# LayerNorm of the tokens along partitions, on a host-transposed copy, in place of TensorE's token transpositions

## What is computed

```python
def _layernorm(x, axis=-1, eps=1e-05):
    m = jnp.mean(x, axis=axis, keepdims=True)
    v = jnp.var(x, axis=axis, keepdims=True)
    return (x - m) / jnp.sqrt(v + eps)
...
q = (x @ w_q)   # of _layernorm(x)
k = (context @ w_k)
v = (context @ w_v)
sim = jnp.einsum('bhid,bhjd->bhij', q, k) * SCALE
out = einsum('bhij,bhjd->bhid', softmax(sim), v)
...
x = x + _L0_xattn_ref(_layernorm(x, axis=-1), ctx_768, L0_xattn_w_q, L0_xattn_w_k, L0_xattn_w_v, L0_xattn_w_o, L0_xattn_b_o)
x = x + _L0_ffn_ref(_layernorm(x, axis=-1), L0_ffn_gate, L0_ffn_W1, L0_ffn_b1, L0_ffn_W2, L0_ffn_b2)
```

## Time and profile before

| | |
|---|---|
| median of 3 runs | 1581.21 us (1580.75 to 1581.81) |
| the profiled execution | 1580.22 us, its span 1578.5 us |
| PE busy | 1553.8 us, 98% |
| PE weight load | 1454.0 us, 92% |
| DVE busy | 1176.1 us, 75% |
| ACT busy | 1108.0 us, 70% |
| POOL busy | 818.1 us, 52% |
| mean TensorE clock granted | 0.994 |
| moved by DMA | 145.05 MB, 92 GB/s |

### The profile page before, as it was taken

The page is one execution under the profiler, slowest core; times in us unless marked ns, Lnnn a source line. Parts: engine busy times, 40 slices in busy tenths (PEclk is TensorE's granted clock), DMA queues, the critical chain, the costliest instruction groups (busy, mean ns, idle before and its releaser), DMA issues.

```text
span 1578.5 us, 45424 instructions
## 1 busy us (share of the span) xinstructions
PE 1553.8 (98%) x14150; PEld 1454.0 (92%) x14151; DVE 1176.1 (75%) x3796; ACT 1108.0 (70%) x3357; POOL 818.1 (52%) x946
## 2 busy tenths in 40 slices
PE   8999999999999999999999999999999999999997
PEld 7899999999899999999999989998899999999997
DVE  4777777777777777777777777777788777777775
ACT  5677677677776777767767777676666676777774
POOL 2344545545554554554555455455456555555556
PEclk9999999999999999999999999999999999999999
DMA  6522111222111221211122211122799755555554
GB/s 201 145 72 74 60 60 60 77 90 72 62 60 60 67 94 66 74 60 60 63 75 89 74 60 60 60 67 81 241 231 249 144 86 85 89 86 90 84 84 61
DMA packets 105643, 145.05 MB, mean 92 GB/s; under 512 B 12736, under 2 KB 87616, under 8 KB 105344
## 3 DMA queue, kind: packets, MB, share of 16 engines
q1 hardware_dynamic: 60144, 89.00, 17.8%
q0 software_dynamic: 26816, 37.32, 13.7%
q10 hardware_dynamic: 18640, 18.19, 4.4%
HBM read 77.09 MB, written 67.38 MB: 92 GB/s over the span
## 4 chain that ended last, share of the span: by engine, by line
issue 47%; POOL 22%; PE 9%; DVE 7%; DMA 6%; DVEq 3%; ACT 2%; POOLq 2%; ACTq 1%; SPq 0%
POOL lists L662 7%; DMA out<-stage_room,number 6%; PE bank_a L1404 4%; POOL prob L669 3%; DVE hid L1332 3%; POOL rstd L648 2%; DVE stage_room L1349 2%; POOL stage_room L711 2%; POOL stage_room L707 2%; POOL out L735 2%; DVEq L1344 1%; PE bank_v L1437 1%; POOLq L729 1%; PE bank_s L1422 1%; DVEq L1323 1%
## 5 line engine op out<-in xcount | busy, mean ns | idle before, releaser
L669 POOL TENSOR_TENSOR prob<-prob,inv 128x512 f32<-128x512 f32 x256 | 271.4, 1060 | 520.3 <-DVE inv L956 519.6
L777 ACT ACTIVATE prob<-bank_s,low 128x128 f32<-128x128 f32 x1024 | 363.3, 376 | 40.9 <-DVE low L951 40.9
L735 POOL DMA_INDIRECT out<-stage_room,number x142 | 231.8, 1632 | 53.9 <-issue 53.1
L951 DVE TENSOR_REDUCE low<-bank_s 128x4 f32<-128x512 f32 x256 | 175.4, 685 | 98.0 <-PE bank_s L1422 97.9
L777 ACT ACTIVATION_READ_ACCUMULATOR prob<-bank_s,low 128x1 f32 x1024 | 221.1, 216 | 0.0
L770 ACT ACTIVATE probt<-bank_t 128x512 f32<-128x512 f32 x256 | 153.4, 599 | 89.6 <-PE bank_t L1411 89.6
L1050 DVE SCALAR_TENSOR_TENSOR stage_room<-xin,wo_t 128x256 f32<-128x256 f32 x480 | 178.8, 426 | 0.0
L807 ACT ACTIVATE ot_h<-bank_v 128x512 fp32r<-128x512 f32 x128 | 77.4, 604 | 138.4 <-PE bank_v L1437 138.4
L885 ACT ACTIVATE hidt_h<-hid 128x512 fp32r<-128x512 f32 x142 | 89.7, 632 | 117.4 <-DVE hid L1332 112.2
L1411 PE MATMUL bank_t<-ident,prob 128*128 128x128 f32 x1024 | 161.9, 281 | 4.0 <-POOL prob L669 4.0
L1404 PE MATMUL bank_a<-xt_l,wq_h 128*128 128x256 f32 x512 | 152.4, 298 | 0.3 <-DVE xt_l L966 0.3
(11 more groups left out here) (231 smaller groups left out, 4728.9 us busy)
## 6 DMA issues: line engine op xcount, KB each, us to landing
stage_room<-lists ACTq DMA_DIRECT2D x67, 265.0 KB
halves<-stage_room SPq DMA_DIRECT2D x32, 512.0 KB
homes<-halves SPq DMA_DIRECT2D x16, 1024.0 KB, 6.4
xin<-in_x SPq DMA_DIRECT2D x32, 256.0 KB, 2.8
stage_room<-in_x SPq DMA_DIRECT2D x32, 256.0 KB
stage_room<-in_w SPq DMA_DIRECT2D x32, 256.0 KB, 4.3
out<-stage_room SPq DMA_DIRECT2D x32, 256.0 KB, 2.2
cin<-in_ctx SPq DMA_DIRECT2D x32, 128.0 KB, 2.6
```

Source lines behind the costliest of these rows:

```text
L669: pool.tensor_tensor(prob[:, n % 4, :, :], prob[:, n % 4, :, :], wide(inv[:, n % 4, :], P), ALU.mult).then_inc(s_norm.sem, 1)
L735: pool.indirect_dma_start(out, bass.IndirectOffsetOnAxis(ap=number[:, u, b:b + 1], axis=0), ysum[:, u, b, :], None, compute_op=ALU.add).th ...
L777: e = act.activation(prob[:, n % 4, h, :], bank_s[n % 2][:, h * P:(h + 1) * P], ACT.Exp, bias=low[:, n % 4, h:h + 1], scale=-1.0, accum_ou ...
L951: dve.tensor_reduce(low[:, n % 4, :], bank_s[n % 2][:, :].rearrange("p (h k) -> p h k", h=4), AX.X, ALU.min).then_inc(s_low.sem, 1)
```

## The change

The host hands over a second, transposed copy of the tokens, `x_t`. SP loads it for each pair into `xraw` (features on partitions). Statistics and `rstd` are made as before, from `xin`, with `rstd` written into `mean_var` beside the mean. As mean and `rstd` are now wanted along the free axis on all partitions, SP writes the 2 x 2 numbers of each partition to DRAM (`ln_rows`) and reads them back broadcast to all partitions as `ln_all` (128x512: per token block and token the mean and `rstd`, so that the mean of one token lies four elements from that of the next). DVE then subtracts and multiplies over `xraw`, two instructions of 128x512, in slot 3, ahead of emptying o1; ACT copies `xraw` to `xt_h` in slot 4, behind `copy_t` and ahead of `exps`; DVE takes the low part from `xraw` in slot 4 where it took it from the bank. t0 is gone, and with it one of 16 users of `bank_a`; the banks now stand in a table. In the first iteration PE spreads the statistics by four products with `ident` instead.

```diff
     A_SLOTS = [
...
-        [("o1", FROM0), ("t0", NEXT)],
+        [("o1", FROM0)],
...
+    BANK_OF = {"q10": 0, "k10": 1, "o0": 2, "k11": 3, "q11": 0, "o1": 1, "v10": 2, "v11": 3,
+               "q00": 0, "k00": 1, "q01": 2, "k01": 3, "v00": 1, "f0": 0, "v01": 2}
...
+            def ln_through(sp, it):
+
+                if not isinstance(it, int) or it > 0:
+                    sp.wait_ge(ln_in, it * 16)
+                wait(sp, pool_step, it, "rstd1")
+                sp.dma_start(ln_rows, mean_var[:, 0, :, :]).then_inc(ln_out, 16)
+                sp.wait_ge(ln_out, it * 16 + 16)
+                wait(sp, xn_step, it - 1, "xn")
+                sp.dma_start(ln_all.rearrange("p t b k -> p (t b k)"), ln_rows.rearrange("t b k -> (t b k)").rearrange(
+                    "(o n) -> o n", o=1).to_broadcast([P, 4 * P])).then_inc(ln_in, 16)
...
+                    sp.dma_start(xraw.rearrange("p c b t -> p c (b t)"),
+                                 x_t[:, cols].rearrange("(c p) t -> p c t", p=P)).then_inc(xt_in, 16)
...
                         wait(sp, c_lo, it - 1, "c")
-                        wait(sp, ln1_step, it - 1, "ln1")
+                        wait(sp, xa_lo, it - 1, "x")
+                        wait(sp, ln1_step, it - 1, "bn1_1")
...
                         load_x(it)
+                        ln_through(sp, it)
...
+                        if n == 4 and has(it, NEXT):
+
+                            wait(act, a_full, it, "q11")
+                            wait(act, xn_step, it, "xn")
+                            act.activation(xt[0][:, 0:DC, :], xraw.rearrange("p c b t -> p c (b t)"),
+                                           ACT.Copy).then_inc(xa_hi.sem, 1)
...
+                def of_tokens(it, k):
+
+                    if isinstance(it, int) and it == -1:
+                        rows_wide = bank_s[1][:, 2 * k * P:(2 * k + 2) * P].rearrange("p (b t) -> p b t", b=2)
+                    else:
+                        rows_wide = ln_all[:, :, :, k].rearrange("p t b -> p b t")
+                    return rows_wide.rearrange("p (o b) t -> p o b t", o=1).to_broadcast([P, DC, 2, P])
+
+                def normalise_turned(it):
+                    dve.wait_ge(xt_in, (it + 2) * 16)
+                    if isinstance(it, int) and it == -1:
+                        dve.wait_ge(ln_first, 1)
+                    else:
+                        dve.wait_ge(ln_in, it * 16 + 16)
+                    dve.tensor_tensor(xraw[:, :, :, :], xraw[:, :, :, :], of_tokens(it, 0), ALU.subtract).then_inc(xn_step.sem, 1)
+                    wait(dve, xn_step, it, "centred")
+                    dve.tensor_tensor(xraw[:, :, :, :], xraw[:, :, :, :], of_tokens(it, 1), ALU.mult).then_inc(xn_step.sem, 1)
+
+                def low_of_tokens(it):
+                    wait(dve, xa_hi, it, "x")
+                    dve.tensor_tensor(xt[1][:, 0:DC, :], xraw.rearrange("p c b t -> p c (b t)"),
+                                      xt[0][:, 0:DC, :].bitcast(F32), ALU.subtract).then_inc(xa_lo.sem, 1)
...
+                        if n == 3 and has(it, NEXT) and not (isinstance(it, int) and it < 0):
+                            normalise_turned(it)
...
+                        if n == 4 and has(it, NEXT):
+                            low_of_tokens(it)
                         made_in = it - 1 if n == 0 else it
...
-                        if n == 1 and has(it, NEXT):
-                            normalise(it, 0, xin, [xn[:, 0, :], xn[:, 1, :]])
...
-                        if k == 0:
-                            wait(pe, a_done, it if g == 0 else it - 1, "t0")
+                        if name == "q00":
+                            wait(pe, xa_lo, it, "x")
```

More of the change, by code:

```diff
@@ L130, in program @@
         [("o1", FROM0)],
[L131 removed]
+        [("v10", CUR), ("v11", CUR)],
         [],
@@ L225, in program @@
             cin = place("cin", 2, 2 * P)
-            xn = place("xn", 2, D)
-            place("not_used", WORK + HOME - taken_to[0])
+            xraw = place("xraw", DC, 2, P)
+            ln_all = place("ln_all", P, 2, 2)
+            assert taken_to[0] == WORK + HOME
             qt = place("qt", 2, CHUNKS // 2, 2 * P)
@@ L359, in by_products, with a_bank @@
                 return isinstance(it, int) and it < 1
[L361 to L367, removed]
+            def a_bank(name):
+                return bank_a[BANK_OF[name]]
             def bank_before(it, name):
+                same = [n for n, _ in A_EVENTS if BANK_OF[n] == BANK_OF[name]]
                 if not isinstance(it, int):
[L372 to L376, removed]
+                    k = same.index(name) - 1
+                    return (it if k >= 0 else it - 1), same[k]
+                order = [(j, n) for j in range(-1, PAIRS + 1) for n in a_full.present(j) if n in same]
+                k = order.index((it, name)) - 1
                 return order[k] if k >= 0 else (it, None)
@@ L647, in rstd_of @@
                     wait(pool, pool_step, it, f"shift{k + 1}")
-                    pool.tensor_tensor(rstd[:, k, :], shifted[:, k, :], mhalf[:, :],
+                    pool.tensor_tensor(mean_var[:, 0, :, 1] if k == 0 else rstd[:, k, :], shifted[:, k, :], mhalf[:, :],
                                        ALU.pow).then_inc(pool_step.sem, 1)
@@ L958, in second_part @@
                 def second_part(it, name):
-                    src = a_bank(it, name)
+                    src = a_bank(name)
                     kind, k = name[0], int(name[-1])
[L961 to L968, removed]
+                    wait(dve, a_full, it, name)
+                    if kind == "v":
                         last = dve.tensor_copy(vv[:, int(name[1]), k, :], src[:, :])
@@ L1035, in rows_of @@
                     dve.wait_ge(sent, (it - 1) * 64 + 16)
-                    normalise(it, 1, x1, [rows[:, b, 0:D] for b in range(2)])
+                    normalise(it, x1, [rows[:, b, 0:D] for b in range(2)])
                 def x_scores(it, first, many):
@@ L1128, in body @@
                             wait(dve, ln1_step, it, "bn1_1")
+                            if not isinstance(it, int) or it > 0:
+                                dve.wait_ge(ln_out, it * 16)
+                            elif it == 0:
+                                dve.wait_ge(ln_first, 1)
                         if n == 4 and has(it, PREV):
@@ L1448, in product @@
                         wait(pe, a_hi if of[0] in "qk" else a_done, earlier, of)
[L1449 to L1455 removed]
+                    if kind == "q":
                         g = int(name[1])
[L1457 to L1458 removed]
+                        if name == "q00":
+                            wait(pe, xa_lo, it, "x")
                         for j in range(2):
@@ L1567, in keep_busy, with first_statistics @@
                                   skip_group_check=True)
+                def first_statistics():
+                    wait(pe, pool_step, -1, "rstd1")
+                    pe.wait_ge(made, 20)
+                    for k in range(2):
+                        for b in range(2):
+                            last = pe.matmul(bank_s[1][:, (2 * k + b) * P:(2 * k + b + 1) * P],
+                                             mean_var[:, 0, b, k:k + 1].to_broadcast([P, P]), ident[:, :],
+                                             start=True, stop=True, skip_group_check=True)
+                    last.then_inc(ln_first, 1)
                 def gate_means():
@@ L1587, in _ @@
                 keep_busy(3)
-                pe.wait_ge(made, 20)
+                first_statistics()
                 iterations(pe, body)
```

56 lines of the change are left out of this document (26 added, 30 removed).

## The result

The changed kernel takes 1593.28 us at the median of 6 runs (1589.35 to 1595.74), the kernel before 1581.71 us beside it (1580.75 to 1582.68): a ratio of 1.0072, 95% interval 1.0058 to 1.0085. It is slower. The profiled execution took 1589.35 us, its span 1587.6 us against 1578.5 us. It is the fastest of the six runs, so of the 11.6 us between the medians its trace can account for some 9.

The account below looks back on a forecast made before the run. PE was taken to bound the loop: 0.86 us stall minus 0.44 us gained gives +0.42 us, 12.6 us over 30 iterations; with 0.6 us at the start 1593.4 us profiled, 1594.4 us median; range 1576 to 1613 us.

Parts of the forecast that it names:

- its own sign: Prediction counts as wrong if ACT gets to the tokens' high part before 2.28 us after u4's scores, or idle time stands elsewhere.
- the stall: PE before k00, waiting for the context's low part from DVE: 0.86 us an iteration, bounds 0.6 and 1.0 us.
- Bottleneck: Attention loop: PE is busy throughout, so work leaving its stream saves time and any wait of PE adds time.
- t0's worth: PE between an output sum's last product and `values`: 0.44 us an iteration gained, 31 x 0.44 = 13.6 us.
- The transfers: Statistics' DRAM round trip in the loop: 2.8 us each way, 2.3 us room, costed at nothing; `xraw` load at start, 0.6 us.
- Slot 3: DVE's subtraction and multiplication before o1: 0.60 us each from start to start, plus waiting with POOL; o1 0.15 to 0.2 us late.
- S: Zero point of the times within an iteration: the start on PE of the scores for u4 and u5.
- Exclusion with POOL: DVE with two SBUF operands and POOL reading SBUF exclude each other; the later waits, as with a `norm` of 1.04 us.
- The late high part: ACT, slot 4: tokens' high part starts behind `copy_t` 2.28 us after u4's scores, ends at 2.91, delaying DVE's low part and k00.
- S's: Wait before u3's transposes, by the experiments' theory that DVE's slot 3 is too long through 16-byte step and exclusion with POOL.
- the restart: PE at k00: the first product behind a wait takes 0.11 us more, 0.39 against the usual 0.28 us.
- rival A: Slot 3: four-element stride makes both DVE instructions 1.22 us, transposes 1.2 us late; 1606 us, or 1624; chance 0.20.

Follow-up runs that it names:

- the best version: Changed kernel with statistics 8 bytes apart, slot 3 of DVE free of gate products (X_SCORES 1: (0, 11), 2: (11, 3), 5: (14, 2)), high part early: 1571.15 us, ratio 0.9938.

## Why the prediction came out as it did

The time was right, 1594.4 against 1593.28 us (for the profiled execution 1593.4 against 1589.35 us); by what it was made of, half of it was not. By its own sign, idle time that stands elsewhere than before k00, its account of the stall is wrong.

- **Bottleneck, and t0's worth: right.** PE had no slack, `values` moved up by 0.44 us an iteration, an iteration in which nothing waits takes 33.73 us instead of 34.16, and the best version gets 9.9 of the 13.6 us.
- **The transfers: right.** Costed at nothing in the loop, and nothing waits for them: the write and its wait took 1.5 us at the median where 2.8 was put. At the start the first minimum came 0.30 us later (23.60 to 23.90), where 0.6 was put.
- **Slot 3: the step that failed.** "A `tensor_tensor` of this size takes DVE 0.60 us from start to start": taken from rows whose operands lie side by side. With one operand read 16 bytes apart it takes 1.07 us, and 1.10 us from start to start (0.70 and 0.69 us at 8 bytes apart). The forecast had o1 0.15 to 0.2 us late; it was 0.83 us late (660.82 against some 659.99, 0.32 behind its last product as in the kernel before). The minimum came at S + 2.14 instead of the forecast's S + 1.56. The exclusion was in the sum and the step was not; with the step taken away, or the exclusion, the wait before the transposes is gone.
- **Exclusion with POOL: right.** The multiplication of 1.85 us that is 1.08 us without `norm` shows it, as does `norm` itself: 1.53 us beside the low part.
- **The late high part: right and hidden.** It came at S + 2.28 as forecast (663.19). Its wait before k00 appears wherever S's is taken away, with 0.38 to 0.54 us of idle time. It is smaller than forecast because the minimum of u4 is earlier there, at S + 1.3 to S + 1.5 and not at S + 1.56: in the kernels with 8 bytes, with the products moved, with the short `norm` and with slot 3 free and the high part late, k00 starts 4.98 or 4.99 us behind that minimum (S + 6.30 behind S + 1.32 up to S + 6.49 behind S + 1.50). Behind S + 1.56 this gives S + 6.54, where the forecast had it before the restart (6.49 and 0.05). The term was sized right, but for a slip of 0.03 us: 6.49, 0.05 and 0.11 make S + 6.65 and not S + 6.62, which is 0.9 us of the time.
- **Where the stall sits: wrong; rival A's place.** It is the wait before the transposes, which come 0.68 us late; 0.75 us is lost by k00. The context's low part, which ends at S + 6.02 (666.25 and 0.68), is late behind it unseen. That 0.75 us came out beside the forecast's 0.86 is the luck of two errors: one delay missed, and the other hidden by it.
- **Rival A: right in kind, too large in size.** It took the step to cost a doubling, 1.22 us, and asked for 1606 us. A step of 16 bytes makes it 1.07 us in place of 0.69, and this is what the Trainium skill ("SBUF — State Buffer", "Door 1: The DMA port swizzle", the note on cachelines) lets one expect: a penalty for going to another 16-byte line each time, and with 8 bytes, where two neighbours share a line, there is none left (0.70 us). The trace agrees with the direction of the rule; its size is read from the runs. The same note gives four float32 elements as how far one can stride for free; read as a step of four, that is not what was measured.

## What to carry to other kernels

Cost an added instruction by a row that has its access pattern and its operands' places, not only its number of elements; where no row has the pattern, that is the widest bound of the sum. When a wait is forecast, ask which other delay would end earlier in the same stream and hide it: an edit that removes one of two stacked delays gains only their difference, and each has to be tested with the other gone. A change that frees the bottleneck by moving work to another engine pays only if that work's neighbours in the queue are rearranged with it; here 1593 us became 1571 us by two such moves (gate products and high part) and by statistics laid 8 bytes apart.

## What the runs showed of the hardware that was not expected

- DVE, 128x512 in float32, two operands in SBUF: 1.07 us (1056 to 1073 ns on the mean, by kernel) with one of them read 16 bytes apart, 0.70 us at 8 bytes apart.
- A write of 2 KB to DRAM and the wait for it take 1.5 us at the median of 31 iterations in pieces of 16 bytes (1.4 to 3.1), and 3.1 us in pieces of 8 bytes (2.8 to 4.3).
- Instructions of ACT and DVE that wait for TensorE's results started 0.45 to 1.3 us later than elsewhere behind the same records of TensorE, in one place of the iteration, in kernels that differ from undisturbed ones by one move on ACT or DVE. No cause was found.
